# Dummy products of TensorE ahead of its wait for the copied score maxima in a fused decoder layer

## What is computed

```python
x = x + self_attn(layernorm(x))        # one head of 128, softmax over each row's top 32 scores
x = x + cross_attn(layernorm(x), ctx)  # 16 heads of 8 features, softmax over 128 keys
x = x + ffn(layernorm(x))              # 8 experts, one chosen per row by argmax(x @ centroids.T)
```

## Time and profile before

| | |
|---|---|
| runs of the kernel before | 446.05, 446.96, 453.71 us; median 446.96 |
| the profiled execution | 450.14 us, with a span of 448.4 us |
| TensorE busy | 408.6 us (91%) |
| VectorE, ScalarE, GpSimd busy | 302.5, 235.8, 203.4 us |
| mean granted clock of TensorE | 0.949 |

### The profile page before, as it was taken

The page is one execution under the profiler, slowest core; times in us unless marked ns, Lnnn a source line. Parts: engine busy times, 40 slices in busy tenths (PEclk is TensorE's granted clock), DMA queues, the critical chain, the costliest instruction groups (busy, mean ns, idle before and its releaser), DMA issues.

```text
span 448.4 us, 12918 instructions
## 1 busy us (share of the span) xinstructions
PE 408.6 (91%) x4209; PEld 291.2 (65%) x4209; DVE 302.5 (67%) x1203; ACT 235.8 (53%) x523; POOL 203.4 (45%) x356
## 2 busy tenths in 40 slices
PE   5898679999999999999999999999979999999990
PEld 5676544545555555555556565756779999999980
DVE  7789815796877887887788675565364056666660
ACT  1464116576757757767656654435400177677750
POOL 7767300310620680680480572561786124445451
PEclk9999959999989989989989999999996999999996
DMA  5112211242222232132111131010002533333310
GB/s 131 41 24 68 48 30 19 49 139 48 66 78 48 62 92 50 42 126 59 27 39 38 24 103 20 13 39 1 25 26 80 156 86 97 97 99 97 95 53 0
DMA packets 30418, 27.33 MB, mean 61 GB/s; under 512 B 6019, under 2 KB 25607, under 8 KB 30352
## 3 DMA queue, kind: packets, MB, share of 16 engines
q1 hardware_dynamic: 25696, 19.32, 17.1%
q0 software_dynamic: 2784, 6.37, 4.2%
q10 hardware_dynamic: 1872, 0.81, 0.7%
HBM read 14.73 MB, written 8.01 MB: 51 GB/s over the span
## 4 chain that ended last, share of the span: by engine, by line
PE 65%; issue 8%; ACT 8%; SPq 7%; DVE 5%; POOL 4%; DMA 1%; DVEq 0%; ACTq 0%; POOLq 0%
PE s_bank L1403 13%; PE s_bank L349 7%; SPq L494 6%; PE pvt_bank L1430 6%; PE att_bank L360 5%; PE s_bank L1363 5%; PE self_bank L360 3%; PE s_bank L1408 3%; PE cross_bank L1358 3%; PE cross_bank L1353 3%; ACT weights L1159 2%; PE s_bank L1392 2%; PE att_bank L1446 2%; PE att_bank L1593 2%; PE pvt_bank L1371 2%
## 5 line engine op out<-in xcount | busy, mean ns | idle before, releaser
L884 DVE TENSOR_REDUCE neg_hmax<-s_bank 128x4 f32<-128x512 f32 x128 | 82.8, 684 | 56.8 <-PE s_bank L1392 56.2
L1159 ACT ACTIVATE weights<-s_bank 128x512 f32<-128x512 f32 x128 | 69.5, 595 | 80.1 <-PE s_bank L1408 69.0
L1392 PE MATMUL s_bank<-k_room,q_room 32*128 32x512 f32 x256 | 93.2, 675 | 2.9 <-ACT hmax_t L1150 2.9
L1403 PE MATMUL s_bank<-q_room,k_room 32*128 32x512 f32 x256 | 76.9, 678 | 6.5 <-DMA q_room<-q_room 6.5
L692 POOL TENSOR_TENSOR x<-x_bv,attended 128x128 f32<-128x128 f32 x32 | 14.6, 455 | 123.8 <-DVE attended L911 123.5
L425 POOL DMA_INDIRECT out<-x_in,q_room x39 | 37.8, 970 | 52.7 <-DVE x_in L389 52.7
L1430 PE MATMUL pvt_bank<-weights,xv 128*32 128x128 f32 x1024 | 48.2, 288 | 2.6 <-ACT weights L1159 1.6
L375 DVE TENSOR_TENSOR q_room<-s_bank,b_cols 128x512 f32<-128x512 f32 x39 | 27.0, 691 | 29.4 <-PE s_bank L349 28.0
L1363 PE MATMUL s_bank<-ident 128*128 128x128 f32 x300 | 42.0, 304 | 2.0 <-POOL ident_bf L654 2.0
L1363 PEld LDWEIGHTS s_bank<-ident 128*128 128x128 f32 x300 | 40.5, 219 | 2.5 <-POOL ident_bf L654 2.0
L349 PE MATMUL s_bank<-k_room,self_room 128*128 128x128 f32 x312 | 41.3, 275 | 0.0
(11 more groups left out here) (193 smaller groups left out, 782.7 us busy)
## 6 DMA issues: line engine op xcount, KB each, us to landing
q_room<-routed_rows SPq DMA_DIRECT2D x39, 130.0 KB, 2.1
w<-in_w SPq DMA_DIRECT2D x16, 256.0 KB
x_in<-in_x SPq DMA_DIRECT2D x8, 256.0 KB, 3.4
ctx_in<-in_ctx SPq DMA_DIRECT2D x8, 256.0 KB, 3.0
k_room<-k_room SPq DMA_DIRECT2D x128, 16.0 KB
q_room<-q_room SPq DMA_DIRECT2D x128, 16.0 KB
routed_rows<-blank SPq DMA_DIRECT2D x5, 130.0 KB
out<-x_in,q_room POOLq DMA_INDIRECT x39, 2.3
```

The costliest lines, as they stand in the source:

```text
L884: dve.tensor_reduce(neg_hmax[:, first:first + 4], bank.rearrange("p (h k) -> p h k", k=S), AX.X, ALU.max, negate=True).then_inc(s["s1_max" ...
L1159: act.activation(weights[:, u, :], s2_bank[:, (u % 2) * GS:(u % 2 + 1) * GS], ACT.Exp, scale=HEAD_SCALE).then_inc(s["s2_exp"], 1)
L1392: pe.matmul(s1_bank[:, (u % 2) * GS:(u % 2 + 1) * GS], natural(q_nat, g, j, strip(u)), masked(k_masked, K_RING, g, j, strip(u)), start=Tru ...
L1403: pe.matmul(s2_bank[:, (u % 2) * GS:(u % 2 + 1) * GS], natural(k_nat, g, j, u), masked(q_masked, Q_RING, g, j, u), start=True, stop=False)
```

## The change

Ahead of the wait for `hmax_t_ready` in `s1` of strip 1, `keep_awake(4, 2)` is called. The condition takes in batches 2 to 31, so it is issued 30 times, in each odd step that still has an `s1` to make, from step 1 of group 0 to step 3 of group 7.

```diff
                 if u == 1 and later(G * g + j, 1):
+                    if g >= 0 and G * g + j > 1:
+                        keep_awake(4, 2)
                     pe.wait_ge(s["hmax_t_ready"], G * g + j)
                 pe.matmul(s1_bank[:, (u % 2) * GS:(u % 2 + 1) * GS], natural(q_nat, g, j, strip(u)), masked(k_masked, K_RING, g, j, strip(u)),
                           start=True, stop=True).then_inc(s["s1_done"], 1)
```

## The result

The changed kernel takes 484.88 us (median of 4 runs, 484.13 to 485.66), against 446.63 us for the kernel before (median of 4, 446.05 to 453.71): 1.086 times as long, with a 95% interval of 1.083 to 1.088. The forecast was 478 us with a range of 466 to 489.

What follows compares the result with a forecast made beforehand. TensorE was taken to bound the loop: 450.1 us profiled, plus 40.5 for issue order, less 4 coming back, less 5.6 for clock dips, gives 481.0; less 3.2 for the median, 478 us, range 466 to 489.

Steps and rivals of the forecast that it cites:

- What bounds the kernel: Main loop: TensorE, busy 408.6 of 448.4 us, sets the pace and VectorE follows, waiting 46.5 us for `s1`.
- The length and place of the dummies: Odd steps, between `s1` of strip 0 and strip 1: 32 records take 1.0 us, starting at T+1.05.
- T: Start of the first `s2` score product in a step; other times in the step are counted from it.
- The lone product and the next work at T+3.07: Odd steps: `s1` of strip 1 starts at T+2.05, runs alone for 1.02 us, then the next work starts.
- The kinds of places: The 30 places, grouped by present distance to the next work, pay 0.38 to 1.77 us each, together 40.5 us.
- What comes back: About 12 places where `pv` stands for its weights: exponentials start with the shift, some 0.3 us each, 4 us off.
- The clock: Behind step 5 of groups 1 to 4: filled idle time ends four half-clock dips, giving back 5.6 us.
- The sum: Whole kernel: 450.1 us profiled + 36.5 - 5.6 = 481.0 us; 478 us for the median, 3.2 us lower.
- Rival A: Clock in the loop: the half-clock dips stay, 484 us, or four more come, 489 us; chance 0.17.
- B: Dummies in odd steps run partly in the shadow of the four score products: 452 us, halfway 465; chance 0.12.
- C: Loop: TensorE has hidden slack, so dummies fill time waited anyway; 439 us, 2% faster at most; chance 0.03.
- D: The `keep_awake` call: only one set of four dummies, 0.2 us long, is issued; 457 us; chance 0.02.

## Why the prediction was right, and one step wrong

The account for the loop, against the one without clock dips (240.45 us, the 8 calls in step 5), is 42.0 us, or 40.5 against the second profile of that version; against the loop before, 36.5, so the dips gave back 5.5.

- What bounds the kernel: right. TensorE sets the pace of the loop, and doubling the dummies added 94% of their length.
- The length and place of the dummies: T+1.05 to T+2.05 forecast, T+1.06 to T+2.07 measured. The reason I gave for the start was too short, as the one-strip kernels show, but the number held.
- The lone product and the next work at T+3.07: measured T+3.12. Over the 30 places the small differences make up 1.5 us: 42.0 and not 40.5 us.
- The kinds of places: right. In the changed kernel all 30 have the next work at T+3.12 or so, save one that waits for the exponentials.
- What comes back: wrong, and the one step that failed. I had 4 us coming back because the exponentials would start with the shift, which moves less than TensorE's next work. They do not start with the shift. They start at T+3.29, behind the lone product that stands ahead of the shift in the program, and so move by 1.91 in step 3 where TensorE's next work moves by 1.83. Nothing came back. The Trainium skill, page TensorE: Matmul & The Clock Gate, section Part 3: Packing small matmuls — row/col tiling, says that matmuls start and end strictly in program order; this trace agrees (T+3.29), and so does the kernel with the shifts first (T+1.38). The trace of the kernel before has the row for it, in step 5 of group 3 (T = 187.01), which I had not read:

```profile
189.87 1.09 ACT L1159 ACTIVATE weights<-s_bank 128x512 f32<-128x512 f32 x2 [1.33 <-PE s_bank L1408]
```

There the exponentials start at T+2.86, behind the lone product, though the shift was issued at T+1.68.
- The clock: the outcome right, the reason in part. The four dips are gone, 5.5 us where 5.6 was forecast. That the size fits is luck in part, since the loop in the second profile of the kernel before stood 14.5 us over the one without dips; against it the changed one is only 27.6 us longer. And the reason, idle time filled, is not enough: the version with the shifts first filled it too, and its dips stayed.
- The sum: in the loop +36.5 in place of +30.9; 4.0 of the 5.6 us between them is the give-back, 1.5 the next work. Between the medians the kernel lost 38.25 us, some 2 us more than the loop did. I subtracted 3.2 us since the profiled execution of before lay so far above its median; that of the changed kernel lies 0.6 us below its own. Which part of that is dips that a usual run of before lacks stays open.

Rival A had the right side and price (484) by the wrong cause: its dips did not come. B, cheap dummies, was true of another form of dummy only, and C of five places only. D had the length of one set of four calls at 0.2 us; such a set is eight records and took 0.36, and with it the product starts at T+1.42 and not T+1.25.

## What to carry to other kernels

Before putting filler work ahead of a wait, look in the timeline whether the engine stands there at all: here it did so in 5 places of 30, and only there did the filler pay, with a length that ends when the wait would. What it gave back was clock and not time of waiting: the next work came at T+2.69 with it and without it. Look also at what runs side by side across that point. Products over different strips run as one pack, and anything in another form between them costs its own length and here up to 0.8 us more for the product that drops out; an instruction put behind a late product also reports late.

## What the runs showed of the hardware

- Products over 32 partitions run beside each other in program order also when others stand between them: one on strip 1 started at T+0.98 among the shifts of strips 2 and 3.
- A dummy on a strip of its own started beside the pack at T+0.02 with 128 output columns, and at T+1.06 with blocks of 32 columns.
- 16 dummy calls a step over one strip (32 x 32) left the loop at a mean clock of 0.95, the same number over all 128 partitions at 1.00, with the same length of 1.07 us; one profile each, not taken side by side.
- Behind step 5 of groups 1 to 4 the clock stayed full in both profiles with 0.57 us of full-height dummies in place of the 0.53 us of idle time; with 0.36 us of dummies and 0.16 us of waiting it fell in three of the four places, as it did in all four in both profiles of the kernel before. With the shifts ahead of the product, no dummies and 0.30 us of waiting it fell in two; with the shifts and 0.36 us of dummies ahead of the product, and no wait, it fell in all four. With full-width dummies on the free strip and 0.41 us of waiting it fell in one of the four.
